# Early expert tiles written by token and finished in token order, in a two-layer kernel with routed experts

## The reference

```python
def _L1_attn_ref(X, W_in, b_in, W_out, b_out):   # s
    QKV = einsum('bsd,ed->bse', X, W_in) + b_in;  Q, K, V = split(QKV, 3)
    Q, K = rope(Q), rope(K)
    A = sum over tokens of (K / |K|) * V
    return einsum('bsd,ed->bse', A * Q, W_out) + b_out + X
def _L1_ffn_ref(x, router_w, gate_w, up_w, down_w):   # silu of this is g
    route = sigmoid(x @ router_w);  max_ind = argmax(route);  max_prob = max(route)
    for e in range(8):
        h = silu(x @ gate_w[e]) * (x @ up_w[e])
        out += where(max_ind == e, h @ down_w[e], 0)
    return out * max_prob
```

## Time and profile before

| | us |
|---|---|
| median of the runs | 355.24 |
| the profiled execution | 354.38 |
| its span, first to last instruction | 352.3 |
| PE busy | 317.4 (90%) |
| DVE busy | 228.8 (65%) |
| ACT busy | 158.8 (45%) |
| POOL busy | 67.2 (19%) |

### The profile page before, as it was taken

The page is one execution under the profiler, slowest core; times in us unless marked ns, Lnnn a source line. Parts: engine busy times, 40 slices in busy tenths (PEclk is TensorE's granted clock), DMA queues, the critical chain, the costliest instruction groups (busy, mean ns, idle before and its releaser), DMA issues.

```text
span 352.3 us, 4819 instructions
## 1 busy us (share of the span) xinstructions
PE 317.4 (90%) x1602; PEld 186.9 (53%) x1602; DVE 228.8 (65%) x498; ACT 158.8 (45%) x289; POOL 67.2 (19%) x85
## 2 busy tenths in 40 slices
PE   3877799999999999999999999999897999999380
PEld 3555565555564544565554565466544677665160
DVE  3997859777675767878957731298983664554541
ACT  1486424775766555634664655323144222232110
POOL 5008650000020000000000013004122200137771
PEclk9999999999999999999999999999999999999956
DMA  7900037064370910000000061079349910314420
GB/s 259 387 0 2 0 75 170 1 131 114 85 161 3 202 40 3 0 1 3 1 3 0 0 182 60 0 271 367 125 120 392 434 73 2 122 59 135 144 82 4
DMA packets 17691, 37.11 MB, mean 105 GB/s; under 512 B 1821, under 2 KB 14334, under 8 KB 16384
## 3 DMA queue, kind: packets, MB, share of 16 engines
q1 hardware_dynamic: 15712, 32.55, 29.2%
q0 software_dynamic: 1952, 4.22, 3.7%
HBM read 33.76 MB, written 13.12 MB: 133 GB/s over the span
## 4 chain that ended last, share of the span: by engine, by line
PE 69%; DVE 16%; issue 4%; DMA 4%; ACT 4%; POOL 2%; POOLq 0%; DVEq 0%; ACTq 0%
PE ps L1710 11%; PE ps L1655 9%; PE ps L1623 8%; PE ps L1723 8%; PE ps L1645 7%; PE ps L1762 5%; PE ps L1528 3%; PE ps L1778 3%; DVE nmax L1203 3%; PE ps L1790 2%; PE ps L1562 2%; PE ps L1827 2%; PE ps L1507 2%; DMA x<-in_x 1%; DVE bn L1068 1%
## 5 line engine op out<-in xcount | busy, mean ns | idle before, releaser
L1203 DVE TENSOR_REDUCE nmax<-ps 128x1 f32<-128x512 f32 x128 | 85.6, 688 | 34.9 <-PE ps L1623 34.3
L940 ACT ACTIVATE shared<-ps 128x512 f32<-128x512 f32 x128 | 74.1, 594 | 53.5 <-PE ps L1645 52.6
L1623 PE MATMUL ps<-experts 96*128 96x512 bf16 x128 | 48.2, 384 | 1.6 <-DVE experts L1210 1.1
L1645 PE MATMUL ps<-experts 99*128 99x512 bf16 x128 | 48.3, 382 | 0.0
L1723 PE MATMUL ps<-shared,experts 128*128 128x256 f32 x128 | 37.5, 386 | 0.0
L1655 PE MATMUL ps<-shared,experts 128*32 128x512 f32 x256 | 34.1, 605 | 0.3 <-ACT shared L940 0.3
L1623 PEld LDWEIGHTS ps<-experts 96*128 96x128 bf16 x128 | 12.5, 98 | 36.7 <-DVE nmax L1203 18.1
L1762 PE MATMUL ps<-experts,shared 128*128 x88 | 24.3, 425 | 5.0 <-ACT shared L1015 5.0
L1723 PEld LDWEIGHTS ps<-shared,experts 128*128 128x128 f32 x128 | 23.4, 190 | 8.9 <-issue 2.5
L948 ACT ACTIVATE experts<-ps 96x1024 bf16<-96x1024 bf16 x18 | 17.9, 1019 | 12.1 <-PE ps L1562 12.0
L1528 PE MATMUL ps<-late_weights,xnT 128*128 128x512 f32 (+1 forms) x64 | 22.5, 492 | 0.4 <-DVE shared L1115 0.4
(11 more groups left out here) (231 smaller groups left out, 527.6 us busy)
## 6 DMA issues: line engine op xcount, KB each, us to landing
experts<-in_experts SPq DMA_DIRECT2D x8, 1536.0 KB, 11.7
slot_rows<-in_empty SPq DMA_DIRECT2D x4, 2080.0 KB, 12.0
shared<-in_wgu SPq DMA_DIRECT2D x1, 2048.0 KB, 10.9
x<-in_x SPq DMA_DIRECT2D x2, 512.0 KB, 5.4
shared<-in_wdn SPq DMA_DIRECT2D x1, 1024.0 KB, 12.8
token_rows<-x SPq DMA_DIRECT2D x1, 1024.0 KB, 15.6
token_rows<-gx SPq DMA_DIRECT2D x1, 1024.0 KB, 4.5
xs<-slot_rows SPq DMA_DIRECT2D x6, 130.0 KB, 2.1
```

What stands on the lines that cost most here:

```text
L940: nc.scalar.activation(probs[:, n % 2, hh, :], ps[:, 2 + hh % 2, :], ACT.Exp, scale=float(HD) ** -0.5).then_inc(s["exp_done"], 1)
L1203: nc.vector.tensor_reduce(nmax[:, 4 * t + hh:4 * t + hh + 1], ps[:, m % 2, :], AX, ALU.max, negate=True).then_inc(s["max_done"], 1)
L1623: nc.tensor.matmul(ps[:, m % 2, :], qs[0:KS, b, GR * g + hh, P * t:P * t + P], ks[0:KS, b, g, :], start=True, stop=True).then_inc(s["score ...
L1645: nc.tensor.matmul(ps[:, 2 + hh % 2, :], ks[0:KM, b, g, P * t:P * t + P], qs[0:KM, b, GR * g + hh, :], start=True, stop=True).then_inc(s[" ...
```

## The change

The results of tiles 0 to 5 (`EARLY` = 6) no longer wait in `held`. `result` leaves them in the small double buffer `ysb`, and POOL scatters each by token to a new DRAM table `expert_results` (`store_early`). When all six have landed, SP loads the table back in token order in four parts of two rows per partition (`yg`), DVE does product and sum for each part (`tokens`), and SP stores the parts to the output with plain DMAs. Tiles 6 and later are gathered and scattered in slot order as before; the first such scatter waits until the four plain stores have landed, since they write every token's row, and the table is filled with zeros beforehand (1 MB, while layer 1 runs). The gather of tile i+3 now stands behind the scatter of tile i. `gathered` gets its own memory, so SP loads the slot rows of tiles 11 to 14 without waiting for scatters.

Three things near the first tiles move as well: PE reads the number of the first expert ahead of the last qkv product; ACT copies the third q transpose ahead of the first result's tanh and does the second sequence's squares in two halves; and DVE runs `sum_tiles(0)` behind the result of tile 0, not ahead of it. POOL's `store_early(0)` stands ahead of the second `key_norms`.

```diff
@@ -47,9 +47,8 @@
...
-HELD = SURE
+EARLY = 6
 GATHERED = 4
-GATHER_AHEAD = 2
@@ -341,11 +340,10 @@
...
-DVE_BETWEEN = {1: [("sum_tiles", 0)], 3: [("branch", 0)], 4: [("sum", 1)], 5: [("branch", 3)]}
-DVE_AFTER = {0: [("rope", 1), ("product", 1)], 2: [("sum", 0), ("sum_tiles", 1)], 3: [("branch", 1)], 4: [("branch", 2)]}
-ACT_AFTER = {0: [("squares", 0)], 1: [("q_T", 2), ("squares", 1)]}
-FINALS = {SURE - 1: (0, 1, 2), SURE: (3, 4, 5), SURE + 1: (6, 7)}
-FINALS_LEFT = {SURE: (3, 4, 5, 6, 7), SURE + 1: (6, 7)}
+DVE_BETWEEN = {3: [("branch", 0)], 4: [("sum", 1)], 5: [("branch", 3)]}
+DVE_AFTER = {0: [("rope", 1), ("product", 1)], 1: [("sum_tiles", 0)], 2: [("sum", 0), ("sum_tiles", 1)], 3: [("branch", 1)], 4: [("branch", 2)]}
+TOKENS = {SURE: (0, 1), SURE + 1: (2, 3)}
+TOKENS_LEFT = {SURE: (0, 1, 2, 3), SURE + 1: (2, 3)}
@@ -355,6 +353,8 @@
...
+    y_dram = nc.dram_tensor("expert_results", (TOK, D), F32, kind="Internal").ap()
+    y_rows = y_dram.rearrange("(p j) d -> p j d", p=P)
@@ -471,8 +471,8 @@
...
-        held = Sa[:, 4096:6144].rearrange("p (j n) -> p j n", j=HELD)
-        gathered = x[:].rearrange("p (a c) n -> p a (c n)", a=GATHERED)
+        yg = Sa[:, 0:2048].rearrange("p (j n) -> p j n", j=NT)
+        gathered = Sa[:, 4096:6144].rearrange("p (a n) -> p a n", a=GATHERED)
@@ -689,6 +692,8 @@
...
+                if u == EMPTYINGS:
+                    sp.dma_start(y_rows, empty_in[:, 0:D].rearrange("p (o d) -> p o d", o=1).to_broadcast([P, NT, D])).then_inc(s["y_cleared"], 16)
@@ -731,22 +736,17 @@
...
-            def reload_rows(i):
-                if i + XR < MT:
-                    sp.wait_ge(s["xs_T"], i + 1)
-                    sp.wait_ge(out_store[i % GATHERED], 16 * (i // GATHERED + 1))
-                    load_rows(i + XR)
-
-            for i in range(SURE):
-                reload_rows(i)
-            n_tiles = sp.value_load(tiles_n[0:1, 0:1], min_val=SURE, max_val=MT)
-
-            def all_loaded(n):
-                for i in range(n, min(n + XR, MT)):
-                    sp.wait_ge(x_sem[i % XR], 16 * (i // XR + 1))
-
-            tiles_from(sp, n_tiles, SURE, reload_rows, all_loaded)
-
+            for a in range(2):
+                sp.wait_ge(y_store[a], 16 * (EARLY // 2))
+            for q in range(NT // 2):
+                sp.dma_start(yg[:, 2 * q:2 * q + 2, :], y_rows[:, 2 * q:2 * q + 2, :]).then_inc(result_sem[q], 16)
+            for i in range(MT - XR):
+                load_rows(i + XR)
+            for q in range(NT // 2):
+                sp.wait_ge(s["tokens_done"], q + 1)
+                sp.dma_start(out[:, 2 * q:2 * q + 2, :], x[:, 2 * q:2 * q + 2, :]).then_inc(token_sem[q], 16)
+            for i in range(MT - XR, MT):
+                sp.wait_ge(x_sem[i % XR], 16 * (i // XR + 1))
@@ -815,39 +815,55 @@
...
+            def store_early(i):
+
+                pool.wait_ge(s["y_ready"], i + 1)
+                nc.gpsimd.indirect_dma_start(
+                    out=y_dram[:, :], out_offset=by_token(i), in_=ysb[:, i % 2, :], in_offset=None, bounds_check=TOK - 1, oob_is_err=False
+                ).then_inc(y_store[i % 2], 16)
...
-                if i >= GATHERED:
-                    pool.wait_ge(out_store[i % GATHERED], 16 * (i // GATHERED))
+                n, a = divmod(i - EARLY, GATHERED)
+                if n:
+                    pool.wait_ge(out_store[a], 16 * n)
                 pool.wait_ge(x_sem[i % XR], 16 * (i // XR + 1))
                 nc.gpsimd.indirect_dma_start(
-                    out=gathered[:, i % GATHERED, :], out_offset=None, in_=xg_dram[:, :], in_offset=by_token(i),
-                    bounds_check=TOK - 1, oob_is_err=False).then_inc(gather_sem[i % GATHERED], 16)
+                    out=gathered[:, a, :], out_offset=None, in_=xg_dram[:, :], in_offset=by_token(i),
+                    bounds_check=TOK - 1, oob_is_err=False).then_inc(gather_sem[a], 16)
...
             def store(i):
-                if i + GATHER_AHEAD < MT:
-                    gather(i + GATHER_AHEAD)
-                pool.wait_ge(s["out_ready"], i + 1)
+                if i == EARLY:
+                    for q in range(NT // 2):
+                        pool.wait_ge(token_sem[q], 16)
+                pool.wait_ge(s["out_ready"], i - EARLY + 1)
+                a = (i - EARLY) % GATHERED
                 nc.gpsimd.indirect_dma_start(
-                    out=out_rows[:, :], out_offset=by_token(i),
-                    in_=gathered[:, i % GATHERED, 0:D], in_offset=None, bounds_check=TOK - 1, oob_is_err=False
-                ).then_inc(out_store[i % GATHERED], 16)
+                    out=out_rows[:, :], out_offset=by_token(i), in_=gathered[:, a, 0:D], in_offset=None, bounds_check=TOK - 1, oob_is_err=False
+                ).then_inc(out_store[a], 16)
+                if i > EARLY and i + GATHERED - 1 < MT:
+                    gather(i + GATHERED - 1)
...
-                for i in range(n, min(n + GATHER_AHEAD, MT)):
-                    pool.wait_ge(gather_sem[i % GATHERED], 16 * (i // GATHERED + 1))
+                for i in range(n, min(n + GATHERED - 1, MT)):
+                    m, a = divmod(i - EARLY, GATHERED)
...
                 for a in range(GATHERED):
-                    pool.wait_ge(out_store[a], 16 * ((n + GATHERED - 1 - a) // GATHERED))
+                    pool.wait_ge(out_store[a], 16 * ((n - EARLY + GATHERED - 1 - a) // GATHERED))
...
+            pool.wait_ge(s["y_cleared"], 16)
+            store_early(0)
             key_norms(1, pool, nc.gpsimd, chain)
             pool.sem_inc(s["norm_ready"], 1)
+            for i in range(1, EARLY):
+                store_early(i)
             pool.wait_ge(s["x_stored"], 16)
             pool.wait_ge(s["g_stored"], 16)
-            for i in range(GATHER_AHEAD):
+            for i in range(EARLY, EARLY + GATHERED):
                 gather(i)
-            for i in range(SURE):
+            for i in range(EARLY, SURE):
                 store(i)
             n_tiles = pool.value_load(tiles_n[0:1, 0:1], min_val=SURE, max_val=MT)
@@ -907,11 +923,12 @@
...
-            def key_squares(b):
-                for j in range(TB * b, TB * b + TB):
+            def key_squares(b, j0, j1):
+                for j in range(TB * b + j0, TB * b + j1):
                     act.wait_ge(s["rope_q"], b + 1)
                     chain(nc.scalar.activation(squares, qkv1[b][:, j % TB, D:2 * D], ACT.Square, accum_out=st1[:, 2, j:j + 1]))
-                nc.scalar.activation(st1[:, 3, TB * b:TB * b + TB], st1[:, 2, TB * b:TB * b + TB], ACT.Copy).then_inc(s["ksum_sq"], 1)
+                if j1 == TB:
+                    nc.scalar.activation(st1[:, 3, TB * b:TB * b + TB], st1[:, 2, TB * b:TB * b + TB], ACT.Copy).then_inc(s["ksum_sq"], 1)
@@ -1029,10 +1046,17 @@
...
                 if i == 2:
                     q_copy(3)
+                    key_squares(1, TB // 2, TB)
                 if i + 1 < MT:
                     xsT_copy(i + 1)
+                if i == 0:
+                    key_squares(0, 0, TB)
+                if i == 1:
+                    q_copy(2)
                 if i:
                     result_tanh(i - 1)
+                if i == 1:
+                    key_squares(1, 0, TB // 2)
@@ -1044,11 +1068,6 @@
...
-                for kind, n in ACT_AFTER.get(i, ()):
-                    if kind == "squares":
-                        key_squares(n)
-                    elif kind == "q_T":
-                        q_copy(n)
@@ -1395,40 +1414,39 @@
...
+                if 2 <= k < EARLY + 2:
+                    dve.wait_ge(y_store[k % 2], 16 * (k // 2))
                 nc.vector.tensor_scalar_mul(ysb[:, k % 2, :], ps[:, 6, 0:D], slot_row(k, PROB_COL, PROB_COL + 1)).then_inc(s["y_half"], 1)
-                if k < HELD:
...
-                    nc.vector.scalar_tensor_tensor(held[:, k, :], ytanh, 1.0, ysb[:, k % 2, :], ALU.add, ALU.mult).then_inc(s["y_ready"], 1)
+                    nc.vector.scalar_tensor_tensor(ysb[:, k % 2, :], ytanh, 1.0, ysb[:, k % 2, :], ALU.add, ALU.mult).then_inc(s["y_ready"], 1)
                     return
-                row = gathered[:, k % GATHERED, :]
+                n, a = divmod(k - EARLY, GATHERED)
+                row = gathered[:, a, :]
                 dve.wait_ge(s["y_half"], k + 1)
-                dve.wait_ge(gather_sem[k % GATHERED], 16 * (k // GATHERED + 1))
+                dve.wait_ge(gather_sem[a], 16 * (n + 1))
...
-                dve.wait_ge(s["product_ready"], k + 1)
+                dve.wait_ge(s["product_ready"], k - EARLY + 1)
...
-            def final(k):
-
-                row = gathered[:, k % GATHERED, :]
-                dve.wait_ge(s["y_ready"], k + 1)
-                dve.wait_ge(gather_sem[k % GATHERED], 16 * (k // GATHERED + 1))
-                nc.vector.tensor_tensor(row[:, D:2 * D], held[:, k, :], row[:, D:2 * D], ALU.mult).then_inc(s["product_ready"], 1)
-                dve.wait_ge(s["product_ready"], k + 1)
```

(39 more changed lines are left out.)

3 lines of the change are left out of this document (2 added, 1 removed).

## The result

The change takes 345.12 us, the median of four runs (344.68 to 346.88), against 355.35 for the kernel before beside it (four runs, 354.95 to 359.5): ratio 0.970, 95% interval 0.962 to 0.978. The forecast was 345.2 us. Two later measurements of the same kernel gave 344.37 and 345.02 us. The profiled execution took 345.08 us, its span is 343.3 us.

What follows compares the result with a forecast made beforehand. Bound by the tail, where POOL's one-by-one gathers and scatters make DVE late, and by PE's waits at the first tiles. 355.24 less 10.0 us (3.6 first tiles, 6.4 tail) gives 345.2 us; range 343.3 to 349.3.

Steps and rivals of the forecast that it cites:

- The first number, 0.85 us: PE ahead of the first gate product: reading the first expert's number earlier gains 0.85 us of 1.41 idle.
- The first tiles together, 3.6 us: Tiles 0 to 2: earlier expert number and new list order start a down product at 269.9, not 273.48; gain 3.6 us.
- Rival A: First tiles: no gain, since the stall only moves or scatter 0 lands too late; 348.5 us, chance 0.10.
- Early scatters and clearing for nothing: POOL's six early scatters, landing in 2.2 to 3.8 us, and the 1 MB of zeros to the table cost nothing.
- The table's loads, last landing near 313: SP's four loads of the table, issued at 307.9: 2.4 us each, the last landing near 313 beside the gathers.
- the 2.6 us: Table loads by the skill page's 2.0 us fixed plus bytes at 436 GB/s: 2.6 us per part, end 0.2 us later.
- Rival C: Tail: parts land late, DVE and PE stand still, PE's clock halves; slower than before from 12 us after issue; 359, chance 0.04.
- DVE: DVE from tile 6 on: parts 0 and 1 done at 316.0, result 7 at 317.9, parts 2 and 3 at 322.1.
- PE at full clock: PE in the tail: no idle time through tile 9's down product, full clock, last down product done at about 330.
- POOL's chain ends last: Tail on POOL: scatter 6 at 325.3, gather 10 at 328.8, six steps of 1.32 us, gather 13 at 336.8, span end 342.3.
- Rival B: Tail on POOL: indirect DMAs slowed by DVE instructions with two SBUF operands, and a later first landing; 348.9 us, chance 0.11.
- The sum: Whole kernel: span end 342.3, 10.0 us less, 3.6 of it from the first tiles and 6.4 from the tail; 345.2 us.

Runs made afterwards that it cites:

- experiment 6: The change with eight buffers for gathered rows, not four, and all eight gathers ahead of the first output scatter; measured twice: 343.89 us (0.966) and 342.58 us (0.965).
- Experiment 10: The kernel before with DVE's bias addition of 2.55 us issued as three pieces; the scatter beside it took 1.52 us, the kernel 359.19 us in its single run.
- experiments 2: The kernel before with only the edits at the first tiles (first expert's number, order of q copy, squares, tanh and `sum_tiles(0)`); 351.7 us, ratio 0.989.
- experiment 3: The change with just the edits at the first tiles undone, so the tail alone; 348.66 us, ratio 0.981 of the kernel before.
- experiment 7: The change with all four token parts behind tile 8, not two there and two at tile 9; 343.86 us, ratio 0.968 of the kernel before.

## Why the prediction was right, step by step

- **The first number, 0.85 us.** Measured 0.86, alone and in the change.
- **The first tiles together, 3.6 us.** Down product at 269.87, the fall of the clock taken off, for 269.9. As an experiment alone 3.8 us of the median. Rival A is out: PE's stalls did not move on, and the first early scatter held up nothing.
- **Early scatters and clearing for nothing.** Right: no DVE instruction shows a wait for them, and the second key norms waited for ACT's squares (1.39 us behind the first scatter), not for the scatter. DVE then waited 0.57 us for these norms, and PE for nothing. The early scatters landed in 2.4 to 6.6 us, not in at most 3.8, still far from the 12 they had.
- **The table's loads, last landing near 313.** This is the term that was mis-sized: 4.3 to 7.5 us from issue, where I had 2.4 and for all four, with the gathers beside them, 5.1 (307.9 to 313). If the longest was that of the last load, it landed near 317.9 (310.4 + 7.5), or 316.4 less 1.55. I had interpolated between a small load and a store of one MB, each alone, and allowed for the neighbours by eye. By the 2.6 us, an estimate from the Trainium skill's page DMA: Bandwidth & Descriptors (Anatomy of one DMA), it would have been as wrong; the page gives that fit for one DMA issued by GpSimd, and these are four issued by SP, so the prediction should not have used it without saying so. It cost nothing because DVE wanted part 0 at 314.80, 1.4 us after the first landing if that was the shortest (309.1 + 4.3), and the last part only at 321.95. Rival C needed landings 12 us after issue; the worst in any of these profiles was 7.7, and in none with the change's tail does DVE wait for a part.
- **DVE.** Parts 0 and 1 were to be done at 316.0, and were at 317.53 - 1.55 = 315.98; result 7 at 317.9, and was at 317.8; parts 2 and 3 at 322.1, and were at 321.8.
- **PE at full clock.** Right in this execution and in six of the other nine with this tail, but the last down product was done at 332.96 - 1.55 = 331.4, not 330: the issue time of 1.90 us ahead of the last transposes was missing from my walk. It did not count, since POOL ended later still. DVE's last instruction ended at 333.4 for 333.6, but for another reason than the one given: it waited 3.37 us for PE, not for tile 10's rows. PE and DVE finish 12.5 us earlier than in before, not "some 14".
- **POOL's chain ends last.** First scatter 326.39 - 1.55 = 324.8 for 325.3, gather 10 at 328.35 for 328.8, gather 13 at 336.75 for 336.8. That the last agrees to 0.1 us is luck in part: the row began 0.45 us early, and its six steps took 8.40 us, not 7.92, with two of them 1.47 and 1.61 us. Eight buffers show the step: with POOL's list changed and DVE's end where it was (fall taken off), the end moved by 2.6 us. Rival B is out: the DMAs of the tail took 0.99 to 1.04 us, apart from single ones of 1.18 to 1.25 us and one of 1.49 (first profile of experiment 6). Experiment 10 bears out what it rests on, that a long DVE instruction holds up a scatter, but the DVE instructions of the tail are short and seldom under way at that moment.
- **The sum.** The predicted span of 342.3 plus 1.5 us of a later gather 13 (the fall of the clock), less 0.5 for a shorter close (5.0 us from the last issue for 5.5), is the 343.3 measured. That the median of the runs came out within 0.1 us of the forecast owes something to chance: single executions differ by 1.5 us for the clock alone, and nothing in the profile of before showed that. The profile of before has no early fall and that of the change has one, so profile against profile gives only 9.0 us, median against median 10.2.

By the ratios of experiments 2 and 3, 3.9 us are the first tiles and 6.6 the tail, each give or take 1.2 to 1.6. DVE's last instruction ends 10.9 us earlier in spite of the fall (345.86 to 334.94), so 12.5 without it; the span lost 9.0, so 10.6 without it. The difference, 1.9, is what POOL's list took back, 2.5 us (gather 13 starts at 338.30; a last scatter 0.83 us behind DVE would have started at 335.77), less the 0.6 by which the close got shorter.

## What to carry to other kernels

When a change takes waits away from one engine, walk the list of the one that will be last next, instruction by instruction with its fixed price: here the list of indirect DMAs on POOL, at 1.32 us each, gave six steps as 7.9 us, and they took 8.4. Then ask which of them need to stand there at all; a gather for an empty tile was the last instruction of the program, and moving the gathers ahead was worth 2.6 us of the span, while one buffer more was worth nothing. That gain can hide behind the clock: in medians it was 0.5 us in one measurement and 2.4 in the other, and only once POOL's row is gone does a slow last down product cost time. Before comparing starts of two profiles, compare the granted clock and one untouched group early on, and take the difference off.

## What the runs showed of the hardware

- The granted clock can fall between 40 and 50 us, in some executions and not in others of one kernel, with the same 2.2 us of idle time of PE ahead of it. Seven profiles have 0.83 on average there, which cost 1.5 to 1.6 us; one (experiment 3) has 0.71, which cost 2.9.
- Four loads of 256 KB issued within 1.8 us land 4.3 to 7.5 us after issue beside gathers, 3.7 to 5.7 without them; in the latter run the DMA engines were busy for 0.86 to 0.93 meanwhile.
- A POOL scatter that starts while DVE runs a long instruction with two operands in SBUF ends about 0.85 us after that instruction (2.25 us beside one of 2.55 us, in thirteen profiles; 1.52 us beside pieces of 0.90, in one).
- Ahead of the last tile's transposes, behind a branch, PE was idle for 0.3 to 2.7 us with no wait that the profiles show (0.34 in before, 1.90 in the change, 1.01 in experiment 7, 2.68 in experiment 10).
